# Experts fed with their own tokens in tiles of 32 slots, weights staged by GpSimd, key rows zeroed in pieces, one block's query rows loaded behind all key rows

## Chip, core and metric

One Trainium2 chip, one NeuronCore of it. The metric is the device time of one execution in microseconds (us). TensorE (PE) runs at one of two clock levels, 1.2 and 2.4 GHz; the profile gives the granted clock as a share of the higher one.

## What is computed

A transformer layer on x of 2048 tokens x 128, float32: causal attention with 16 heads of 8 (rotary), residual, layer norm; then non-causal attention and a top-1 mixture of 8 experts, with residuals and a last layer norm.

```python
# attention 1 (causal), over S = 2048 tokens, H = 16 heads, D_K = 8
Q, K, V = x@Wq.T, x@Wk.T, x@Wv.T;  Q, K = rope(Q), rope(K)
x = layernorm(x + softmax(mask(Q K^T / sqrt(8))) V @ Wo.T)
# "ffn" block: attention 2 (not causal) and the experts, D = 128, HID = 512, E = 8
t = x + msa(layernorm(x)*ln1_w + ln1_b)
xf = layernorm(t)*ln2_w + ln2_b
e = argmax(xf @ gate_w + gate_b)              # one expert for each token
y = gelu(xf @ w1[e]) @ w2[e]                  # 128 -> 512 -> 128
x = layernorm(x + t + y)
```

## The kernel before

**Stages.** The 2048 tokens are four blocks of 512 (`NB = 4`, `BLK = 512`; a block is `TB = 4` tiles of 128). The head of the program projects Q, K and V of all blocks. Q and K are split into two parts, written to DRAM (`q_scratch`, `k_scratch`), and read back several times as the rows of `query_rows` (`QA`, two blocks at a time) and `key_rows` (`KA`, all tokens). Then attention 1 runs over its query blocks, a short passage prepares attention 2, attention 2 runs over its four query blocks, and a tail does what is left of the last block.

**A step of attention.** A query block has four groups of four heads; a group has one step for each 128 keys (16 steps in attention 2, so 64 steps a block). In a step PE computes two score products (L381, `ps<-query_rows,key_rows`), ScalarE turns them into exponentials (`exps`, L782, two instructions of 128x1024), and PE multiplies the exponentials of the step before with the values (`ps<-probs,values`). The values products have 9 output columns each and are put at four column offsets of the array (0, 32, 64, 96). Three pairs of PSUM banks hold scores, so ScalarE can be fed about one step ahead. At a group's end VectorE copies the sum (`evac`), PE turns it in step 3 of the next group (`turn`), and VectorE normalises (`norm`).

**Work in the shade of attention 2.** While PE runs attention 2 of block qb, it also does the experts of block qb-1 (`side2`, a table from step to work, one PSUM bank, number 7). Steps 5 and 7: output projection; 10: turn of the normalised rows; 11: gate; 13: turn of the one-hot rows; 14 to 17: eight masks, one for each expert (`m_masks`, evacuated by `masks` on VectorE, L1220); from step 20 on (`UNIT_AT`) eight units of eight expert products each, spread over five steps a unit (`m_products`). Every expert is applied to all 512 tokens: VectorE and GpSimd multiply the token columns by the expert's mask in turn (`products`, L1231 and L896), and PE accumulates the eight masked products. So a block takes 64 products of 128x512 in float32, each with a 128x128 weight tile, which SP brings in eight loads of 512 KB through a ring (`expert_weights`, L350). A float32 product shows as two records in the profile. Four ScalarE tanh of 128x512 a block make the gelu. Block 3's experts run alone in the tail (`at_once`).

**The head.** GpSimd first zeroes the unused rows of `key_rows` in two memsets of 32x16384 (L900), then fills `values` with ones, then runs `split_k` for each block; ScalarE's first work waits for GpSimd's first sum. SP's queue waits for the two memsets (`rows_clear`), then puts ones in one row of `key_rows` (`ld_pad`), loads small weights and x, and then for each block b: stores its q and k parts, waits until they have landed, loads that block's key rows (four DMAs of 256 KB), and for b < 2 its query rows (eight DMAs of 128 KB). PE starts attention 1 when the key rows of block 0, the query rows of block 0, `ld_pad` and the shift row (`c_row`, issued by ScalarE) are there. ScalarE's work for block 3 waits for the stores of block 1.

## Time and profile before

| | us |
|---|---|
| median of 3 runs (lowest, highest) | 1318.41 (1308.98, 1332.99) |
| the profiled execution | 1305.86 |
| its span, first to last instruction | 1304.0 |

| engine | busy us | share of the span |
|---|---|---|
| PE matmul | 1097.7 | 84% |
| ScalarE | 775.0 | 59% |
| VectorE | 437.5 | 34% |
| GpSimd | 244.8 | 19% |

The busy share is a mean over stages with different limits, and a matmul's end is modelled, so it says which engine is full only together with the waits of a stage. The granted clock was 0.907 over the span. The rows below have start and duration in us; `[0.34 <-X]` behind a row is idle time before it and what ended it.

### The profile page before, as it was taken

The numbers are of one execution on the slowest core, as the hardware profiler recorded it, in microseconds if no ns is written. First come the engines' busy times: TensorE is split into PE (matmuls) and PEld (weight loads), VectorE is DVE, ScalarE is ACT, GpSimd is POOL, SyncE is SP. The second block draws the span as 40 slices with busy tenths as digits, with TensorE's granted clock in tenths as the row PEclk, the third lists the DMA queues.
The fourth block names the chain that finished last, engine by engine and source line by source line (L and its number), as shares of the span: only waits on it lengthen the run. The fifth ranks groups of instructions, "written<-read, shape, count | busy, mean of one in ns | idle before, by whom it ended". The sixth has DMA issues, their size and how long they took to land.

```text
span 1304.0 us, 22822 instructions
## 1 busy us (share of the span) xinstructions
PE 1097.7 (84%) x9300; PEld 444.8 (34%) x9300; DVE 437.5 (34%) x1074; ACT 775.0 (59%) x874; POOL 244.8 (19%) x274
## 2 busy tenths in 40 slices
PE   3408879899889639999999999899999899996667
PEld 1204334334334213333333333333333333333223
DVE  3541251510520360000434221444321534323765
ACT  0206658779779409999756567766567766562000
POOL 9203111110100000000022221022220022220334
PEclk8758798989999758999889899999999899998789
DMA  4766202000061151001001012001100001110010
GB/s 111 147 107 118 35 33 35 34 2 3 27 87 27 25 98 50 1 2 24 12 17 33 17 33 57 11 25 34 33 26 26 1 25 33 33 33 17 24 49 24
DMA packets 52922, 49.88 MB, mean 38 GB/s; under 512 B 3536, under 2 KB 39248, under 8 KB 52816
## 3 DMA queue, kind: packets, MB, share of 16 engines
q1 hardware_dynamic: 52752, 48.33, 17.9%
q8 instruction: 75, 1.23, 0.4%
q14 instruction: 31, 0.25, 0.1%
q10 hardware_dynamic: 64, 0.07, 0.0%
HBM read 38.56 MB, written 9.44 MB: 37 GB/s over the span
## 4 chain that ended last, share of the span: by engine, by line
PE 74%; DVE 13%; DMA 4%; issue 3%; POOL 2%; ACT 2%; SPq 2%; DVEq 0%; ACTq 0%; POOLq 0%
PE ps L381 71%; PE ps L386 3%; POOL key_rows L900 2%; DMA k_scratch<-parts 2%; ACT probs L782 2%; DMA query_rows<-neg_shift_final 2%; DVE early_late L1220 1%; DVE row_low L1191 1%; DVE early_late L1231 1%; DVE squares_blockdiag L1252 1%; DVE early_late L1260 1%; DVE ln_stats L961 1%; DVE ln_newton L956 0%; DVE ln_newton L954 0%; DVE squares_blockdiag L1253 0%
## 5 line engine op out<-in xcount | busy, mean ns | idle before, releaser
L782 ACT ACTIVATE probs<-ps 128x1024 f32<-128x1024 f32 (+3 forms) x832 | 751.7, 1003 | 327.0 <-PE ps L381 324.9
L381 PE MATMUL ps<-probs,values 128*9 128x256 f32 (+1 forms) x6528 | 443.8, 386 | 7.2 <-DVE q_rotated L1108 7.0
L381 PE MATMUL ps<-query_rows,key_rows 33*128 33x512 f32 (+3 forms) x1664 | 328.6, 462 | 39.4 <-DMA query_rows<-neg_shift_final 30.2
L381 PE MATMUL ps<-early_late,parts 128*128 128x512 f32 x512 | 261.8, 636 | 29.6 <-DVE early_late L1231 28.0
L381 PEld LDWEIGHTS ps<-query_rows,key_rows 33*128 33x128 f32 x1664 | 139.4, 192 | 261.1 <-issue 137.4
L381 PEld LDWEIGHTS ps<-probs,values 128*9 128x9 f32 x6528 | 145.6, 91 | 233.7 <-issue 136.3
L896 POOL TENSOR_TENSOR early_late<-h_cols,early_late 128x512 f32<-128x512 f32 x64 | 74.9, 1173 | 499.9 <-DVE early_late L1220 330.5
L381 PEld LDWEIGHTS ps<-early_late,parts 128*128 128x128 f32 x512 | 90.0, 196 | 154.3 <-issue 143.0
L875 POOL TENSOR_SCALAR_AFFINE_SELECT probs<-probs 128x256 f32<-128x256 f32 x128 | 52.2, 409 | 309.3 <-ACT probs L782 306.9
L896 POOL TENSOR_TENSOR early_late<-early_late 128x512 f32<-128x512 f32 x64 | 74.6, 1166 | 176.6 <-PE ps L381 176.1
L1108 DVE COPY q_rotated<-ps 128x512 f32<-128x512 f32 x32 | 22.1, 691 | 234.3 <-PE ps L381 234.1
L1231 DVE TENSOR_TENSOR early_late<-early_late 128x512 f32<-128x512 f32 x64 | 48.2, 763 | 111.3 <-PE ps L381 111.2
L1231 DVE TENSOR_TENSOR early_late<-h_cols,early_late 128x512 f32<-128x512 f32 x64 | 46.8, 744 | 96.1 <-PE ps L381 95.9
L796 ACT ACTIVATE squares_blockdiag<-squares_blockdiag 128x512 f32<-128x512 f32 x16 | 10.1, 631 | 73.7 <-DVE squares_blockdiag L1254 73.7
L1115 DVE RECIPROCAL recip<-ps 128x16 f32<-128x16 f32 x32 | 8.2, 258 | 92.7 <-PE ps L386 92.6
L1220 DVE CAST early_late<-ps 128x512 bf16<-128x512 f32 x32 | 22.1, 692 | 25.3 <-PE ps L381 25.1
L1191 DVE TENSOR_REDUCE row_low<-ps 128x8 f32<-128x512 f32 x32 | 22.1, 692 | 22.0 <-PE ps L381 21.8
L381 PE MATMUL ps<-early_late,w_attn 128*128 128x512 f32 x32 | 19.1, 753 | 10.1 <-DMA early_late<-in_sin 6.5
L900 POOL MEMSET key_rows<- 32x16384 f32 x2 | 27.5, 13744 | 0.3 <-POOLq L1404 0.3
L381 PE MATMUL ps<-row_bound,parts 8*128 8x512 bf16 x32 | 15.4, 489 | 11.8 <-DVE early_late L1220 10.4
L381 PE MATMUL ps<-squares_blockdiag,blk 128*16 128x512 bf16 x8 | 3.7, 461 | 23.3 <-ACT squares_blockdiag L815 23.3
L381 PE MATMUL ps<-squares_blockdiag 128*128 128x512 bf16 x32 | 13.0, 421 | 11.6 <-DVE row_low L1191 11.0
(137 smaller groups left out, 464.9 us busy)
## 6 DMA issues: line engine op xcount, KB each, us to landing
parts<-in_w SPq DMA_DIRECT2D x32, 512.0 KB, 3.8
query_rows<-q_scratch SPq DMA_DIRECT2D x64, 128.0 KB
key_rows<-k_scratch SPq DMA_DIRECT2D x20, 256.0 KB, 7.3
q_scratch<-parts SPq DMA_DIRECT2D x8, 512.0 KB, 5.8
k_scratch<-parts SPq DMA_DIRECT2D x8, 512.0 KB, 5.7
key_rows<-k_scratch SPq DMA_DIRECT2D x16, 192.0 KB, 7.0
early_late<-in_xT SPq DMA_DIRECT2D x4, 256.0 KB, 5.2
early_late<-in_cos SPq DMA_DIRECT2D x4, 256.0 KB, 5.4
```

The costliest lines, as they stand in the source:

```text
L381: return nc.tensor.matmul(out, l, r, start=start, stop=stop, skip_group_check=True)
L386: last = nc.tensor.transpose(out[0:m, i * P:(i + 1) * P], rows(i), ident[:, :])
L782: nc.scalar.activation(Pr[:, i % 2, 2 * p:2 * p + 2, lo:BLK], score_banks(t, p)[:, :, lo:BLK], ACT.Exp, scale=SCALE).then_inc(s["exp"], 1)
L875: nc.gpsimd.affine_select(out=at, in_=at, compare_op=ALU.is_ge, fill=0.0, base=0, pattern=[[0, 2], [1, P]], channel_multiplier=-1).then_in ...
L896: nc.gpsimd.tensor_tensor(prod[:, n % PSLOTS, :], hT[:, :] if c < TB else hid[:, c - TB, :], ms[:, e, :], ALU.mult).then_inc(m_pp, 1)
L900: link(nc.gpsimd.memset(KA[at:at + ROWS, :].bitcast(F32), 0.0))
L961: ins = nc.vector.bn_stats(st[:, i, :], src[:, i, :])
L1108: copy(accs[:, :], sums).then_inc(s["evac"], 1)
L1191: mark(nc.vector.tensor_reduce(low[:, t, hs], low_bank(b, i, c).rearrange("p (h t) -> p h t", t=NSUB), AX.X, ALU.max), low_taken, 2 * t + ...
L1220: mark(copy(ms[:, e, :], mask_bank(b, e)), m_ms, b * E + e + 1)
L1231: tt(prod[:, n % PSLOTS, :], hT[:, :] if u < TB else hid[:, u - TB, :], ms[:, e, :], ALU.mult).then_inc(m_pd, 1)
L1252: link(tt(t, x, x, ALU.mult))
```

## The change

**Experts.** Tokens are sorted by expert into 768 slots (`SORTED`), in `NT = 24` tiles of `TS = 32` slots, each tile with one expert. On PE `m_ranks` (step 13) replaces the turn of the one-hot rows; VectorE works out each token's slot (`dest`) and each tile's expert (`owner`). GpSimd sends the 512 rows to DRAM in four indirect DMAs (`rows_sent`), SP loads the 768 sorted rows (`sorted_rows`), and PE turns them (steps 24 and 25). Then six rounds of four tiles: `up` (four products with 32 stationary columns, 512 moving), `turn` (four transposes), `down` (16 products with 32 stationary columns, 128 moving), at steps `UP_AT`, +5 and +7. The four tiles of a round stand at column offsets 0, 32, 64, 96. The weights of all experts lie in SBUF (W1 in `parts`, W2 in `early_late`, loaded once by SP, 4 MB); for every round GpSimd reads four tile owners into registers and copies four tiles of w1 and four of w2 to `expert_stage` (in the tail ScalarE copies w1). At the block's end GpSimd stores the results and fetches 512 rows back by four indirect DMAs; VectorE adds them in the next block (`add_experts(qb - 2)`, ahead of `route`). Masks, masked products, and the weight ring are gone.

**Head.** The two memsets are cut into four pieces each of 32x4096; GpSimd does a pair of pieces ahead of each `split_k`. SP's ones in `key_rows` and the query rows of block 1 move behind the key rows of all blocks; three stores of zeros to `z_sorted` are added.

```diff
-UNIT_AT = (20, 25, 30, 36, 41, 46, 52, 57)
-TANH_AT = {28: 0, 33: 1, 38: 2, 44: 3}
+UP_AT = (26, 32, 38, 44, 50, 56)
+SORTED_AT = (24, 25)
+TANH_AT = {at + 2: r for r, at in enumerate(UP_AT)}
+IN_SHADE = side_order(UP_AT, 5, 7)
+AT_END = side_order(tuple(30 + 6 * r for r in range(ROUNDS)), 8, 13)
 # SP
-            sp.wait_ge(rows_clear, 1)
-            for at in (ROWS, HALF + ROWS):
-                sp.dma_start(kaf[at:at + 1, :, :]..., onesf...).then_inc(ld_pad, 16)
                 key_rows(1, slice(0, PAIRS), b * BLK, (b + 1) * BLK, A[1]["k_rows"][b % 2])
-                if b < 2:
+                if b == 0:
                     query_rows(1, b)
+            query_rows(1, 1)
+            sp.wait_ge(rows_clear, 1)
+            for at in (ROWS, HALF + ROWS):
+                sp.dma_start(kaf[at:at + 1, :, :]..., onesf...).then_inc(ld_pad, 16)
+            def sorted_rows(b):
+                sp.wait_ge(m_sent, 16 * TB * (b + 1))
+                sp.dma_start(zsl, z_sorted.rearrange("(r p) d -> p r d", p=P)).then_inc(m_sorted, 16)
 # PE
+            def m_up(b, k, r):
+                pe.wait_ge(m_w1, 4 * (b * ROUNDS + r + 1))
+                side_free(b, k, 2)
+                for g in range(4):
+                    last = mm(ps[g * TS:(g + 1) * TS, side_bank(b, k), :], slots(4 * r + g), w1s[g])
+            def m_down(b, k, r):
+                pe.wait_ge(m_w2, 4 * (b * ROUNDS + r + 1))
+                for c in range(TB):
+                    for g in range(4):
+                        last = mm(ps[g * TS:(g + 1) * TS, side_bank(b, k), 0:D], hTs2[...],
+                                  w2s[g][:, c * P:(c + 1) * P], c == 0, c == TB - 1)
 # GpSimd
+            def rows_sent(b):
+                pool.wait_ge(m_dest, b + 1)
+                for i in range(TB):
+                    nc.gpsimd.indirect_dma_start(out=z_sorted, ..., in_=zb[:, i, :], ...).then_inc(m_sent, 16)
+            def rows_back(b):
+                for r in range(ROUNDS):
+                    mine = [pool.value_load(owner[0:1, t:t + 1], ...) for t in range(4 * r, 4 * r + 4)]
+                    if b < NB - 1:
+                        if r:
+                            pool.wait_ge(m_side, ... ("up", r - 1))
+                        for g, e in enumerate(mine):
+                            nc.gpsimd.tensor_copy(w1s[g], W1[:, bass.ds(e * HID, HID)]).then_inc(m_w1, 1)
+                    if r:
+                        pool.wait_ge(m_side, ... ("down", r - 1))
+                    for g, e in enumerate(mine):
+                        nc.gpsimd.tensor_copy(w2s[g], W2[:, bass.ds(e * HID, HID)]).then_inc(m_w2, 1)
+                ... two stores to y_sorted, wait m_stored, four indirect DMAs back to zb
 # VectorE
+            def experts(b, order, due):
+                ... "up": copy(xg[r % 2], side), gelu_arg(b, r) (2 ops)
+                ... "turn": gelu(b, r) (1 op), copy(hTs2[:, :], side)
+                ... "down": ts(yS[:, r, :], side[:, 0:D], 0.5, None, ALU.mult)
```

SP's queue in the head, before, from block 1's stores on: its key rows, its query rows, and then block 2's stores.

```order
L271 DMA q_scratch<-parts 128x2x512 [waits a1_q_split]
L271 DMA k_scratch<-parts 128x2x512 [waits a1_k_split]
L280 DMA key_rows<-k_scratch 16x8x512 [waits a1_parts_out1]
L280 DMA key_rows<-k_scratch 16x8x512 x3
L288 DMA query_rows<-q_scratch 8x8x512 x8
L271 DMA q_scratch<-parts 128x2x512 [waits a1_q_split]
L271 DMA k_scratch<-parts 128x2x512 [waits a1_k_split]
```

And the end of the same part now, block 3 and what follows it:

```order
L305 DMA q_scratch<-parts 128x2x512 [waits a1_q_split]
L305 DMA k_scratch<-parts 128x2x512 [waits a1_k_split]
L314 DMA key_rows<-k_scratch 16x8x512 [waits a1_k_rows1,a1_parts_out1]
L314 DMA key_rows<-k_scratch 16x8x512 x3
L322 DMA query_rows<-q_scratch 8x8x512 x8
L355 DMA key_rows<-ones_f 1x128x128 [waits rows_clear]
```

The query rows of block 1 moved behind the key rows of block 3, and the ones (`ld_pad`) behind them.

PE in attention 2 beside block 0's experts, before: one step of scores and values, and two masked products behind it.

```order
L381 MATMUL ps<-query_rows,key_rows 128x512 [waits a2_exp]
L381 MATMUL ps<-query_rows,key_rows 128x512
L381 MATMUL ps<-query_rows,key_rows 128x512 [waits a2_exp]
L381 MATMUL ps<-query_rows,key_rows 128x512
L381 MATMUL ps<-probs,values 9x256 [waits a2_exp]
L381 MATMUL ps<-probs,values 9x256 x3
L381 MATMUL ps<-probs,values 9x256 [waits a2_exp]
L381 MATMUL ps<-probs,values 9x256 x3
L381 MATMUL ps<-early_late,parts 128x512 [waits m_prod_dve]
L381 MATMUL ps<-early_late,parts 128x512 [waits m_prod_pool]
```

The same place now, `up` of one round and the start of `down` of the round before one step later (a round's other steps hold only attention):

```order
L422 MATMUL ps<-expert_stage,h_cols 32x512 [waits m_side_taken,a2_norm,m_w1_staged]
L422 MATMUL ps<-expert_stage,h_cols 32x512 x3
L422 MATMUL ps<-query_rows,key_rows 128x512 [waits a2_exp]
L422 MATMUL ps<-query_rows,key_rows 128x512
L422 MATMUL ps<-query_rows,key_rows 128x512 [waits a2_exp]
L422 MATMUL ps<-query_rows,key_rows 128x512
L422 MATMUL ps<-probs,values 9x256 [waits a2_exp]
L422 MATMUL ps<-probs,values 9x256 x3
L422 MATMUL ps<-expert_stage,k_work 32x128 [waits m_side_taken,a2_norm,m_w2_staged]
L422 MATMUL ps<-expert_stage,k_work 32x128 x2
```

In place of one or two wide products behind nearly every step stand groups of narrow ones behind three steps in six, and they wait for GpSimd's copies. GpSimd's queue there, before and now (first round of block 0):

```order
L922 COPY values<-early_late 128x256x8 [waits a2_v_taken]
L896 TENSOR_TENSOR early_late<-h_cols,early_late 128x512 [waits m_mask,v_moved]
L896 TENSOR_TENSOR early_late<-h_cols,early_late 128x512
L896 TENSOR_TENSOR early_late<-h_cols,early_late 128x512 [waits m_mm] x14
L896 TENSOR_TENSOR early_late<-early_late 128x512 [waits m_hid,m_mm] x16
```

```order
L1001 COPY values<-early_late 128x256x8 [waits a2_v_taken]
L944 DMA z_sorted<-z_rows,row_shift 768x128 [waits z_clear,m_dest,v_moved]
L944 DMA z_sorted<-z_rows,row_shift 768x128 x3
L954 TENSOR_LOAD row_shift [waits ld_m,m_owner]
L954 ISA x2
L954 TENSOR_LOAD row_shift
L954 ISA x2
```

Four register loads, four copies of w1 and four of w2 a round took the place of the masked multiplications.

## Rows read from the trace of the kernel before

**Rows 1.** The page, part 4: chain that ended last, its largest lines.

```profile
PE 74%; DVE 13%; DMA 4%; issue 3%; POOL 2%; ACT 2%; SPq 2%; DVEq 0%; ACTq 0%; POOLq 0%
```

**Rows 2.** Windows: us, busy PE, PEld, DVE, ACT, POOL (count), clock, DMA share, GB/s.

```profile
490.37:611.76 121.39, 119.94 (x1300) 47.59 (x1300) 6.52 (x17) 118.79 (x131) 0.00 (x0) 0.97 0.06 15
611.76:803.00 191.24, 183.00 (x1422) 68.36 (x1420) 60.56 (x128) 121.78 (x129) 37.10 (x32) 0.94 0.11 26
...
1185.30:1304.00 118.70, 76.72 (x216) 32.88 (x215) 75.18 (x165) 4.50 (x7) 38.23 (x32) 0.84 0.10 29
```

**Rows 3.** Timeline, steps of attention 2 block 0, without experts.

```profile
509.38 0.73 PE L381 MATMUL ps<-query_rows,key_rows 33*128 33x512 f32 x4
...
510.04 1.05 PE L381 MATMUL ps<-probs,values 128*9 128x256 f32 x16
...
511.02 0.73 PE L381 MATMUL ps<-query_rows,key_rows 33*128 33x512 f32 x4
```

**Rows 4.** Timeline, one step of block 1 with two expert products.

```profile
674.23 0.73 PE L381 MATMUL ps<-query_rows,key_rows 33*128 33x512 f32 x4
...
675.87 1.98 PE L381 MATMUL ps<-early_late,parts 128*128 128x512 f32 x4
...
677.79 0.73 PE L381 MATMUL ps<-query_rows,key_rows 33*128 33x512 f32 x4
```

**Rows 5.** Timeline, block 1: a turn at step 3, and the first mask, end of step 14.

```profile
616.77 0.66 PE L386 MATMUL ps<-ident,q_rotated 128*128 128x128 f32 x4
...
640.00 0.38 PE L381 MATMUL ps<-row_bound,parts 8*128 8x512 bf16 x1
```

**Rows 6.** Groups of instructions by form: busy us, mean ns | idle before.

```profile
L896 POOL TENSOR_TENSOR early_late<-h_cols,early_late 128x512 f32<-128x512 f32 x64 | 74.9, 1173 | 499.9 <-DVE early_late L1220 330.5 <-PE ps L381 169.4
L900 POOL MEMSET key_rows<- 32x16384 f32 x2 | 27.5, 13744 | 0.3 <-POOLq L1404 0.3
L796 ACT ACTIVATE squares_blockdiag<-squares_blockdiag 128x512 f32<-128x512 f32 x16 | 10.1, 631 | 73.7 <-DVE squares_blockdiag L1254 73.7
L922 POOL COPY values<-early_late 128x2048 f32<-128x2048 f32 x1 | 1.9, 1893 | 0.0
```

**Rows 7.** Chain of waits near 87 us: a register load on VectorE's queue; the shift row.

```profile
86.88 0.56 DVEq L1071
87.47 0.20 DVEq L1071
...
89.71 10.64 DMA query_rows<-neg_shift_final
```

**Rows 8.** Timeline of SP's queue in the head: issue times.

```profile
39.88 0.47 SPq L271 DMA_DIRECT2D k_scratch<-parts  x1
45.89 2.60 SPq L280 DMA_DIRECT2D key_rows<-k_scratch  x4
...
74.98 2.51 SPq L280 DMA_DIRECT2D key_rows<-k_scratch  x4
...
103.96 2.51 SPq L280 DMA_DIRECT2D key_rows<-k_scratch  x4
...
117.40 2.48 SPq L280 DMA_DIRECT2D key_rows<-k_scratch  x4
```

**Rows 9.** Windows at the end of the head's transfers (columns as in rows 2).

```profile
117.40:127.00 9.60, 8.99 (x106) 4.48 (x107) 2.73 (x7) 7.72 (x12) 4.61 (x12) 1.00 0.89 110
127.00:134.00 7.00, 2.57 (x40) 1.30 (x32) 1.03 (x4) 1.85 (x4) 1.89 (x5) 0.84 0.03 6
```

**Rows 10.** Timeline of the head: a small VectorE cast while GpSimd zeroes.

```profile
0.80 27.55 POOL L900 MEMSET key_rows<- 32x16384 f32 x2 [0.29 <-POOLq L1404]
...
6.73 7.85 DVE L1346 CAST blk<-blk_f 128x16 bf16<-128x16 f32 x1 [4.75 <-DMA ident<-in_ident]
```

**Rows 11.** Timeline of the tail: the one-hot's turn, the last store.

```profile
1204.98 1.01 PE L386 MATMUL ps<-ident,onehot 128*8 128x128 f32 x4 [2.31 <-DVE onehot L1212]
...
1301.27 0.38 SPq L354 DMA_DIRECT2D out<-x_rows  x1
```

More of the change, by code:

```diff
@@ L638, in group @@
+            side_op = dict(sorted=m_sorted_turn, up=m_up, turn=m_hid_turn, down=m_down)
             def group(a, qb, g, side, after, before):
@@ L706, in after2 @@
                 b = qb - 1
-                first = {0: (m_xadd, b)} if b else {}
-                return {**first, 1: (m_ms, (b + 1) * E), 2: (m_ev, b * 2 * TB + 3), 3: (m_ev, b * 2 * TB + 6)}
+                first = {0: (m_taken, b * OPS)} if b else {}
+                late = {g: (m_taken, b * OPS + sum(at < g * (S // P) + TURN_STEP for at, _, _ in IN_SHADE)) for g in (2, 3)}
+                return {**first, 1: (m_dest, b + 1), **late}
             def side0(a):
@@ L1263, in experts @@
[L1263 to L1275 removed]
+                link(ins)
@@ new lines, in route @@
+                if b == 0:
+                    dve.wait_ge(ld_k, 16)
+                    link(nc.vector.memset(cum[:, 0, :], 0.0))
+                for i in range(TB):
+                    ins = tt(cum[:, i + 1, :], cum[:, i, :], oh[:, i, :], ALU.add)
+                    if i < TB - 1:
+                        link(ins)
+                ins.then_inc(m_oh, 1)
+                dve.wait_ge(m_rank, b + 1)
+                count = ps[:, 7, TB * E:(TB + 1) * E]
+                marks = wide[:, 0:E * BLK // TS].rearrange("p (e k) -> p e k", e=E)
@@ new lines, in experts @@
+            def experts(b, order, due):
+                for k, (at, name, r) in enumerate(order):
+                    if name == "turn":
+                        due(at - 1)
+                        gelu(b, r)
+                    due(at)
+                    n = b * OPS + k + 1
+                    dve.wait_ge(m_side, n)
+                    side = ps[:, side_bank(b, k), :]
+                    if name == "sorted":
+                        c = sorted_cols(r)
+                        mark(ts(c, side[:, 0:c.shape[1]], ln[:, 2:3], ln[:, 3:4], ALU.mult, ALU.add), m_taken, n)
+                    elif name == "up":
+                        mark(copy(xg[r % 2], side), m_taken, n)
+                        gelu_arg(b, r)
+                    elif name == "turn":
+                        mark(copy(hTs2[:, :], side), m_taken, n)
+                    else:
+                        mark(ts(yS[:, r, :], side[:, 0:D], 0.5, None, ALU.mult), m_taken, n)
@@ L1359, in _ @@
             b = NB - 1
+            add_experts(b - 1)
             route(b)
-            masks(b, 0, E)
             finish(b - 1)
-            experts(b, at_once)
+            experts(b, AT_END, at_once)
             add_experts(b)
```

333 lines of the change are left out of this document (170 added, 163 removed).

## Prediction

> **What bounds the kernel now.** I read the page's chain first, then the windows by stage, then the timeline inside a stage. PE holds 74% of the chain [rows 1], so the question is what PE waits for in each stage. Block 0 of attention 2 has no experts beside it: 121.4 us for 64 steps, with ScalarE busy for 118.8 [rows 2]. There ScalarE sets the pace, 118.8 / 64 = 1.86 us a step, while PE alone needs 511.02 - 509.38 = 1.64 us a step [rows 3]. Block 1, with block 0's experts beside it, takes 191.2 us at 121.8 us of ScalarE work and 183.0 of PE [rows 2]: there PE is the bound. A step with two expert products lasts 677.79 - 674.23 = 3.56 us [rows 4], that is 1.64 + 1.92. Blocks 2 and 3 look the same (I count three such blocks at 191.2). The tail of 118.7 us is one block's experts alone. The head, up to the first step of attention 1, is DMA time: the issues of the key rows are 29.1, 29.0 and 13.4 us apart [rows 8], each waiting for stores that stand behind the transfers before.
>
> **The three shaded blocks.** I build the new length of a block from its steps.
>
> Steps 0 to 13 change little. Before they ran from 611.76 [rows 2] to the first mask at 640.00 [rows 5], 28.2 us. `add_experts` puts one VectorE operation of about 0.7 us ahead of `route`, on which PE's turn at step 10 waits, and four small additions (about 0.2 us each) stand ahead of `m_ranks`: 29.7 us.
>
> Steps 14 to 23 held eight masks and the first products; they now hold nothing but the sorting on other engines. Pace of ScalarE: 10 x 1.86 = 18.6 us.
>
> Steps 24 to 63 hold six rounds of six steps. A round adds up, turn and down to PE. Turn: four transposes, 0.6 us [rows 5]. Up: four float32 products of 512 columns, eight records. Two such products (four records) take 1.92 us one behind the other [rows 4], so eight records would be 3.8 us. But the values products, which stand at four column offsets as these do, put 16 records of 256 columns into 0.98 us (510.04 to 511.02 [rows 3]), where serial they would need 16 x 0.24 = 3.8: nearly four at a time. So up is 0.95 us. Down is 16 products of 128 columns in 32 records: overlapped 1.0, serial 32 x 0.12 = 3.8; each needs its own small weight load, so I take 1.6. A round adds 3.15 us.
> The Trainium skill (TensorEngine Tiling (Array Packing), Tiling Modes and Performance Considerations) says that four 128x32 tiles run in parallel, with some 60 cycles of overhead for each product. By it up would be 0.95 as well and down nearer 1.6 than 1.0.
> If PE could always run ahead, a round would be 6 x 1.64 + 3.15 = 13.0 us. With scores only one step ahead I count the three loaded steps at PE's pace (4.9 + 3.15) and the three free ones at ScalarE's (5.6), 13.6 us. Six rounds are 81.6 us; the four steps left over, two turns of sorted rows and the group turns are 8.3, and waits for `evac` behind the gelu operations at steps 33 to 34 about 1.
> Sum: 29.7 + 18.6 + 81.6 + 8.3 + 1 = 139.2 us. Three blocks save 3 x (191.2 - 139.2) = **156 us**. Bounds: 131 (down at 1.0, full run-ahead, no evac wait) and 164 (up and down serial) a block.
>
> This is only so if nobody is late. Two chains have to fit.
> (1) Sorting. The slots are known some 3 us behind step 13. Then come four indirect DMAs from GpSimd, their landing, SP's load of 384 KB, and PE's turn at step 24, ten steps or 19 us later. No row has an indirect DMA. Lower bound: an SP issue, 0.6 us each, 2.5 us for four [rows 8]. Upper bound: 3 us each. I take 1.2: 3 + 4.8 + 2 + 3.5 = 13 us, hidden. At 3 us each it is 20.5 and PE stands 1 to 2 us.
> (2) Staging. GpSimd's copy of 2048 columns took 1.89 us [rows 6], so 512 take about 0.55. A register load on VectorE's queue cost 0.56 + 0.20 = 0.8 us [rows 7]. A round is 4 x 0.8 + 8 x 0.55 = 7.6 us against a window of five steps, about 11 us (down of one round to up of the next but one). Hidden. At 1.17 us a copy, the price of a GpSimd multiplication [rows 6], it is 12.6 and PE would stand about 1.7 us a round.
> ScalarE gets two more tanh a block, 1.3 us at 0.63 [rows 6], hidden while PE bounds. SP has fewer loads; its wait for the sent rows holds up only `rows_out` and the next shift row, due a block later.
>
> **The tail.** The one-hot rows are ready at 1204.98 [rows 11]. Now: add_experts 0.7, counts 0.8, ranks 1.0 (four transposes cost 1.01 there [rows 11]), slots 2.0, four sends 4.8 and landing 2.0, load 3.2, turn and evacuation 2.0: first up at 1221.5. Before, the first product stood at about the same place. Then rounds: w1 has one buffer, so ScalarE starts four register loads and four copies when the last up is done; I take 4 x 1.2 + 1.0 for up = 5.9 us. Last up 1222.5 + 5 x 5.9 = 1252; gelu, turn, down 7.5; store 3.3; fetch 6.8; add 0.7; layer norm 5.1; last store's issue at 1275.5, against 1301.27 before [rows 11]. With the round still open I put **24.5 us** saved; bounds 10 (3 us a DMA, 8 us a round) and 35.
>
> **The head.** GpSimd no longer holds up the start. The two memsets took 27.5 us [rows 6]; with a quarter of them ahead (6.9 us), block 0's stores can be issued when VectorE and ScalarE are through, near 20.5 instead of 39.9 [rows 8]. Later blocks need their split 29 us apart, and 6.9 + 4 us of GpSimd fit. But the transfers remain. Block 0's stores to its key rows 6.0 us; key rows, query rows and stores 29.1; without query rows 13.4; so query rows alone are 15.7, and the last key rows 9.6, when the DMA share falls from 0.89 to 0.03 [rows 8, 9]. Now in a row: 6 + 29.1 + 13.4 + 13.4 + 9.6 + 15.7 = 87.2, and `ld_pad` stands behind all of it, some 3 us. PE waits for `ld_pad` before its first product, so attention 1 starts at 20.5 + 90 = 111 instead of 100.4 (where the shift row landed, 89.71 + 10.64 [rows 7]). Before, block 1's query rows and the keys of blocks 2 and 3 still moved while PE worked. I put **+10.5 us**; bounds -8 (ring rates a fifth better) and +15.
> The Trainium skill (SBUF — State Buffer, "The 'DVE blocks DMA' trap") says that GpSimd and VectorE lock a shared port out for whole instructions. The trace agrees: a cast of 16 columns took 7.85 us and ended with the first memset [rows 10].
>
> **Sum.** 1304.0 - 156 - 24.5 + 10.5 = 1134; 1.9 us lie outside the span: 1136 for an execution like the profiled one (1305.86). The median of the runs shown is 1.0% above that one; I go half of it up and predict **1141 us**.
>
> **Rivals.**
> (A) Staging is late, 15%. Copies at 1.17 us make PE wait 1.7 us in each of 18 rounds (31 us) and sends of 3 us add 5 in the blocks and 9 in the tail. 1141 + 45 = 1186. For it: GpSimd's multiplications run at 1.17 and VectorE gets in its way. Against: a plain copy ran at half of that.
> The Trainium skill (SBUF — State Buffer, the same section) says that DMAs issued from GpSimd starve while VectorE holds that port; no row here has such a DMA, and by it time would move to this rival.
> (B) The narrow products don't overlap: up and down at 3.8 each, 25 us a block and some in the tail, 1141 + 80 = 1221; 5%. Against it: [rows 3].
> (C) The head gains: with the transfers at better rates, or attention 1 quicker since nothing moves beside it, it starts at 92, 19 us below my sum, and the tail is at its best: 1112; 17%.
> (D) Slower than before: GpSimd becomes the bound. To pass 1318 x 1.02 the 24 rounds would have to take 8.5 us more each than in my sum, 13.6 + 8.5 = 22 us for a round of twelve GpSimd operations, 1.85 us each. The dearest row is 1.17, so 3%; then some 1350.
> (E) The experts' saving is eaten elsewhere, within 2%: sorting so late (over 60 us a block) that PE stands. Chain (1) would have to be four times my sum; 2%.
> My forecast has 58%.
>
> **Range.** The forecast's own: blocks 3 x 5, tail 10, head 8, run to run 8; about 1115 to 1170. To hold 8 in 10 it reaches to (C) and towards (A): 1108 to 1178. A difference under 2% can't be told from none in this kernel. Faster 0.95, same 0.02, slower 0.03.
>
> **What would show it.** Three stretches of attention 2 with experts at 136 to 143 us, PE busy over 90% of each at a clock of at least 0.95; steps 14 to 23 at 1.86 us. No PE idle before the sorted turn at step 24 or before up (else A). Up about 1 us for eight records, down 1.6 (else B). GpSimd's copy 0.55. First product of attention 1 near 111, released by the ones of `key_rows`, with SP's first store near 20 (else C). Last up to last store about 23 us. Wrong would be: PE idle behind GpSimd's copies, a clock that falls in the shade, or a block over 165.

## The result, and the profile after

The changed kernel took 1136.11 us in the median of 4 runs (1127.68 to 1151.96), beside 1314.34 us for the kernel before on the same chip: a ratio of 0.863, with a 95% interval of 0.857 to 0.869. Some executions of a kernel are slow ones, over 1.5% above its fastest: the ratios leave them out, and the profiled executions of `spread` (1131.41 us) and `tail_order` (1140.23) are such. The execution profiled has a span of 1125.9 us; the one before had 1304.0. The chain of work that ended last, by engine:

```profile
PE 66%; DVE 11%; DMA 9%; ACT 5%; issue 4%; SPq 2%; POOL 1%; another core or an unknown queue 1%; POOLq 0%; ACTq 0%; DVEq 0%
```

PE has fallen from 74% of the chain [rows 1] to 66% and VectorE from 13% to 11%; the DMAs have risen from 4% to 9%. The windows of the kernel after, by stage (columns as in [rows 2]): the head, attention 1, the passage, attention 2's blocks 0 to 3, the tail.

```profile
0.00:107.60 107.60, 30.03 (x110) 14.96 (x110) 37.27 (x88) 11.96 (x21) 40.47 (x22) 0.67 0.74 149
107.60:452.00 344.40, 308.68 (x3255) 135.42 (x3261) 91.10 (x265) 263.83 (x320) 51.90 (x127) 0.92 0.15 27
452.00:501.60 49.60, 15.94 (x70) 8.60 (x67) 31.34 (x106) 3.49 (x7) 3.51 (x4) 0.65 0.45 81
501.60:623.00 121.40, 119.91 (x1304) 47.74 (x1308) 6.50 (x17) 118.98 (x131) 0.00 (x0) 0.97 0.13 39
623.00:757.20 134.20, 130.40 (x1594) 57.70 (x1586) 43.15 (x117) 122.57 (x135) 35.21 (x54) 1.00 0.08 17
757.20:892.70 135.50, 130.65 (x1596) 57.91 (x1594) 51.03 (x141) 122.62 (x135) 38.95 (x58) 1.00 0.10 20
892.70:1027.70 135.00, 129.84 (x1596) 57.54 (x1594) 51.56 (x141) 121.08 (x133) 38.95 (x58) 1.00 0.04 13
1027.70:1125.90 98.20, 34.91 (x302) 20.56 (x302) 50.07 (x152) 18.34 (x30) 30.93 (x38) 0.56 0.08 23
```

Against [rows 2]: block 0 is the same. The three shaded blocks run from 623.0 to 1027.7, 404.7 us, where they ran from 611.76 to 1185.3, 573.5: **168.8 us saved**. The tail went from 118.7 to 98.2: **20.5 saved**. Attention 1 starts at 107.6 instead of 100.4: **7.2 lost**. Between there and the start of attention 2's block 0 another **4.0** were lost. In all -168.8 - 20.5 + 7.2 + 4.0 = -178.1, the difference of the spans. PE is busy for 96 to 97% of a shaded block, at full clock; in the tail for 36%, at 0.56.

### The profile page after: what moved, and what is told of

It is laid out like the page before. It is cut to its first block, busy times and chain, and to the rows that moved or that the text cites. A ratio compares the mean times of both kernels' runs of the same rounds, so it can differ in the third digit from the quotient of the medians.

```text
span 1125.9 us, 24400 instructions
## 1 busy us (share of the span) xinstructions
PE 900.4 (80%) x9813; PEld 400.4 (36%) x9820; DVE 362.0 (32%) x1027; ACT 782.9 (70%) x906; POOL 239.9 (21%) x360
## 4 chain that ended last, share of the span: by engine, by line
PE 66%; DVE 11%; DMA 9%; ACT 5%; issue 4%; SPq 2%; POOL 1%; another core or an unknown queue 1%; POOLq 0%; ACTq 0%; DVEq 0%
PE ps L422 61%; DMA k_scratch<-parts 4%; ACT probs L829 4%; PE ps L427 3%; DMA key_rows<-ones_f 2%; DVE row_low L1273 1%; PE ps L675 1%; DMA y_sorted<-early_late 1%; DMA query_rows<-neg_shift_final 1%; SPq L322 1%; ACT squares_blockdiag L843 1%; DMA z_rows<-y_sorted,row_shift 1%; POOL z_rows L970 1%; SPq L314 1%
## 5 line engine op out<-in xcount | busy, mean ns | idle before, releaser
L422 PE MATMUL ps<-query_rows,key_rows 33*128 33x512 f32 (+3 forms) x1664 | 337.0, 465 | 73.1 <-DMA key_rows<-ones_f 42.6
L963 POOL COPY expert_stage<-early_late 128x512 f32 x72 | 45.4, 668 | 162.1 <-PE ps L422 162.1
L944 POOL DMA_INDIRECT z_sorted<-z_rows,row_shift x16 | 15.8, 990 | 237.3 <-issue 177.0
L959 POOL COPY expert_stage<-parts 128x512 f32 x72 | 47.9, 707 | 44.6 <-PE ps L422 39.1
L900 ACT ACTIVATE expert_stage<-parts 128x512 f32 x24 | 15.1, 630 | 48.7 <-DVE row_shift L1322 27.6
L1354 DVE COPY k_work<-ps 128x512 f32<-128x512 f32 x24 | 16.6, 690 | 62.9 <-PE ps L675 62.9
L422 PE MATMUL ps<-expert_stage,k_work 128*32 128x128 f32 x576 | 29.3, 301 | 4.1 <-issue 2.4
L422 PEld LDWEIGHTS ps<-expert_stage,k_work 128*32 128x32 f32 x576 | 24.2, 122 | 13.6 <-issue 6.2
L422 PE MATMUL ps<-early_late,w_attn 128*128 128x512 f32 x32 | 19.9, 780 | 11.4 <-DMA early_late<-in_sin 7.3
L422 PE MATMUL ps<-early_late,k_work 128*32 128x128 f32 x192 | 29.0, 301 | 0.0
L984 POOL MEMSET key_rows<- 32x4096 f32 x8 | 28.0, 3504 | 0.9 <-POOL row_ok L974 0.5
L422 PE MATMUL ps<-expert_stage,h_cols 128*32 128x512 f32 x128 | 20.2, 709 | 4.4 <-ACT expert_stage L900 3.3
## 6 DMA issues: line engine op xcount, KB each, us to landing
query_rows<-q_scratch SPq DMA_DIRECT2D x64, 128.0 KB
```

What stands on the lines that cost most here:

```text
L422: return nc.tensor.matmul(out, l, r, start=start, stop=stop, skip_group_check=True)
L900: nc.scalar.activation(w1s[g], W1[:, bass.ds(e * HID, HID)], ACT.Copy).then_inc(m_w1, 1)
L944: nc.gpsimd.indirect_dma_start(out=z_sorted, out_offset=bass.IndirectOffsetOnAxis(ap=dest[:, i:i + 1], axis=0), in_=zb[:, i, :], in_offset ...
L959: nc.gpsimd.tensor_copy(w1s[g], W1[:, bass.ds(e * HID, HID)]).then_inc(m_w1, 1)
L963: nc.gpsimd.tensor_copy(w2s[g], W2[:, bass.ds(e * HID, HID)]).then_inc(m_w2, 1)
L984: link(nc.gpsimd.memset(KA[at:at + ROWS, part].bitcast(F32), 0.0))
```

## Experiments

Ratios are to the kernel before, run beside each, with their 95% interval in brackets; the changed kernel's is 0.863. "Block" is the time from one gate product to the next in the trace: the two shaded stretches are 195.8 and 191.0 us in the kernel before, 135.6 and 135.0 in the changed one, and the stretch from the last shaded one into the tail is 180.4 and 128.0.

### What the blocks' 169 us were: columns on TensorE

`narrow_products`, on the kernel before:

```diff
+                    wide = BLK if e == 0 else P
-                    mm(unit_bank(b, u), wring[:, (n // E) % WSLOTS, e, :], prod[:, n % PSLOTS, :], ...
+                    mm(unit_bank(b, u)[:, 0:wide], wring[:, (n // E) % WSLOTS, e, :], prod[:, n % PSLOTS, 0:wide], ...
```

> The kernel before with seven of every eight expert products on 128 columns instead of 512 (the output leaves out those experts for three quarters of the tokens); masks, masked copies, loads and waits are all there. Theory 1 (the product's columns on TensorE priced the shaded block, 0.86 us each): 56 x 0.64 = 36 us less in each of three blocks and 0 to 25 in the tail, 1312 - 108 - 12 = about 1190 us (1180 to 1215). Theory 2 (the masked copies on VectorE and GpSimd, 1.9 us for two, or the waits for masks carried the block): under 15 us a block, over 1265 us.

It took 1202.96 us, ratio 0.915 (0.909 to 0.921). The gate's products in its timeline:

```profile
801.41 1.06 PE L381 MATMUL ps<-gate_w,h_cols 128*128 128x8 f32 x8
...
962.17 1.06 PE L381 MATMUL ps<-gate_w,h_cols 128*128 128x8 f32 x8
```

They are 160.8 us apart, against 191.0: 30.3 less there and 35.4 in the block ahead, with every masked copy, mask, load and wait in place. So the columns priced the block, at 30 to 35 of the 36 us worked out.

`full_width`, on the changed kernel:

```diff
-                    last = mm(ps[g * TS:(g + 1) * TS, side_bank(b, k), :], slots(4 * r + g), w1s[g])
+                    last = mm(ps[:, side_bank(b, k), :], sorted_cols(r // 4)[:, r % 4 * P:(r % 4 + 1) * P], w1s[g], g == 0, g == 3)
...
-                        last = mm(ps[g * TS:(g + 1) * TS, side_bank(b, k), 0:D], hTs2[:, c * P + g * TS:c * P + (g + 1) * TS],
-                                  w2s[g][:, c * P:(c + 1) * P], c == 0, c == TB - 1)
+                        last = mm(ps[:, side_bank(b, k), 0:D], hTs2[:, c * P:(c + 1) * P],
+                                  w2s[g][:, c * P:(c + 1) * P], c == 0 and g == 0, c == TB - 1 and g == 3)
```

> The changed kernel with each expert product on all 128 columns of its round instead of on its tile's 32: the four products of a step are added up in one bank, so the output is no longer the reference's from there on (each slot gets the sum over its round's four tiles' experts). Same number of products, same columns streamed, but no two of them beside each other. Theory 1 (narrow tiles overlap four times, and TensorE's time carries the block): up goes from 0.97 to 3.4 us, down from about 0.95 to 3.4, so 4.5 to 5 us more in each of 18 shaded rounds and 5 to 9 in the tail's 6 at half clock: 1136 + 85 + 40 = about 1260 us (1230 to 1290), a shaded round 17.5 us instead of 12.9. Theory 2 (ScalarE's pace carries the block, TensorE has room): under 30 us more.

It took 1258.54 us, ratio 0.963 (0.955 to 0.970). Its timeline, two ups of one block:

```profile
703.71 3.70 PE L422 MATMUL ps<-expert_stage,h_cols 128*128 128x512 f32 x8
...
722.25 3.70 PE L422 MATMUL ps<-expert_stage,h_cols 128*128 128x512 f32 x8
```

A round is 18.5 us here. In the changed kernel the same eight records take 1.04 us, and down's 32 take 0.99, from their first at 701.79 to the score product behind them at 702.78:

```profile
699.28 1.04 PE L422 MATMUL ps<-expert_stage,h_cols 128*32 128x512 f32 x8
...
701.79 0.29 PE L422 MATMUL ps<-expert_stage,k_work 128*32 128x128 f32 x3
...
702.57 0.27 PE L422 MATMUL ps<-early_late,k_work 128*32 128x128 f32 x1
702.78 0.73 PE L422 MATMUL ps<-query_rows,key_rows 33*128 33x512 f32 x4
```

The same number of products over the same moving columns, with four beside each other or with none, differs by 122 us. The weights of `full_width` are wider too (128 stationary columns instead of 32), but a record costs 3.70 / 8 = 0.46 us there, no more than one of the old products with the same weights (1.98 / 4 = 0.50 [rows 4]), so it is the overlap that is gone. Without the overlap the change would still have been faster than before, but by 4%.

### What the head's 7 us were: the place of the ones

`before_head` is the kernel before with only the head of the change: the value memset first, the key rows zeroed in pairs of pieces, block 1's query rows and the ones behind all key rows.

> The kernel before with only the head of the change: the values' ones first, key rows zeroed in four pairs of pieces between the key splits, the ones and block 1's query rows behind all key rows. Theory 1 (the prediction's head term): slower by 7 to 11 us, attention 1 starts at 108 to 111 instead of 100.4. Theory 2 (the head term is right but only beside the sorting's other changes, or it is a gain): no change or faster by 5 us and more.

1324.93 us, ratio 1.010 (1.003 to 1.017): a small loss, 12 us by the medians. Attention 1 starts at 110.18, released by the ones. By itself this part of the change costs time.

`query_back`, the changed kernel with block 1's query rows loaded where they were before:

```diff
-                if b == 0:
+                if b < 2:
                     query_rows(1, b)
-            query_rows(1, 1)
             sp.wait_ge(rows_clear, 1)
```

> The changed kernel with block 1's query rows loaded behind block 1's key rows again, as before, the ones still last. Theory 1 (what is behind the ones matters, not the order ahead of them): the sum of transfers ahead of the ones is the same, so within 3 us of the changed kernel, 1133 to 1139 us. Theory 2 (the order of the query rows is what the head's loss or gain comes from): 5 to 10 us more or less.

1132.48 us, ratio 0.864 (0.859 to 0.869): no difference. Attention 1 starts at 104.2, still on the ones. The order ahead of them hardly matters. What they stand behind does:

`pads_early`:

```diff
+                if b == 1:
+                    sp.wait_ge(rows_clear, 1)
+                    for at in (ROWS, HALF + ROWS):
+                        sp.dma_start(... the ones ...).then_inc(ld_pad, 16)
             query_rows(1, 1)
-            sp.wait_ge(rows_clear, 1)
-            for at in (ROWS, HALF + ROWS):
-                sp.dma_start(... the ones ...).then_inc(ld_pad, 16)
```

> The changed kernel, with the wait for the zeroed key rows and the two transfers of ones moved from behind all key rows to right behind block 1's key rows (query rows of block 1 stay behind all key rows). Theory 1, the place of the ones behind everything sets the start of attention 1: in the changed kernel it starts at 107.6 us, the ones issued at 88.5. Issued at about 56 and landing within 3 to 19 us they let it start at 70 to 76, block 0 of attention 1 (24 us) is over at about 97, and block 1 waits for its query rows until about 105 instead of starting at 132: 25 to 32 us less in all, 1104 to 1111 us. Theory 2, the volume of the head's transfers sets it (87 us of them one behind another): attention 1 starts early, but its first blocks wait for rows and less than 10 us are gained, 1126 to 1136 us.

1105.28 us, ratio 0.842 (0.836 to 0.848), **31 us less than the changed kernel** by the medians, 28 by the ratios. First the changed kernel's SP queue and first product of attention 1, then those of `pads_early`:

```profile
53.40 2.50 SPq L314 DMA_DIRECT2D key_rows<-k_scratch  x4
...
87.88 1.26 SPq L355 DMA_DIRECT2D key_rows<-ones_f  x2
```

```profile
107.59 1.54 PE L422 MATMUL ps<-query_rows,key_rows 33*128 33x512 f32 x6 [42.60 <-DMA key_rows<-ones_f]
```

```profile
54.50 2.72 SPq L355 DMA_DIRECT2D key_rows<-ones_f  x2
```

```profile
69.02 1.54 PE L423 MATMUL ps<-query_rows,key_rows 33*128 33x512 f32 x6 [5.47 <-DMA query_rows<-neg_shift_final]
...
108.51 1.22 PE L423 MATMUL ps<-query_rows,key_rows 33*128 33x512 f32 x4 [10.65 <-DMA query_rows<-neg_shift_final]
```

PE stood 42.6 us for two rows of ones whose operands were ready at about 50 (the last memset ends at 49.5); 38.6 of them were the ones' alone, since the shift row lets PE start at 69.0. It is the place that makes them late: behind the eight loads of query rows the second landed 19.0 us after its issue in the changed kernel (88.5 to 107.5), and 9.6 in `pads_early`. Issued early, they let block 0 of attention 1 run beside the other blocks' transfers, and block 1 waits 10.65 us for its shift row, where it waited 4.86 in the changed kernel.

### Staging: hidden, but with little to spare

`stage_twice`:

```diff
+                            link(nc.gpsimd.tensor_copy(w1s[g], W1[:, bass.ds(e * HID, HID)]))
                             nc.gpsimd.tensor_copy(w1s[g], W1[:, bass.ds(e * HID, HID)]).then_inc(m_w1, 1)
...
+                        link(nc.gpsimd.tensor_copy(w2s[g], W2[:, bass.ds(e * HID, HID)]))
                         nc.gpsimd.tensor_copy(w2s[g], W2[:, bass.ds(e * HID, HID)]).then_inc(m_w2, 1)
```

> The changed kernel with every expert weight copy on GpSimd done twice, one behind the other (5.3 us of copies a round become 10.7 to 11, in the three shaded blocks; in the tail only the second weights). Theory 1 (staging is hidden in a round of 12.9 us, and neither its end nor the port it shares with VectorE is on the path): shaded blocks within 2 us of 135 each, the tail 0 to 10 us longer, 1136 to 1146 us. Theory 2 (staging or the shared port is nearly the bound, the prediction's rival A): up or down wait for staged weights, 3 us and more a round, over 1165 us.

1197.92 us, ratio 0.914 (0.909 to 0.919). My theory 1 was wrong here: it is 62 us more. Its timeline, and its windows (columns as in [rows 2]) without a wait and from one up to the next:

```profile
701.76 1.07 PE L422 MATMUL ps<-expert_stage,h_cols 128*32 128x512 f32 x8 [1.36 <-POOL expert_stage L960]
...
717.62 1.94 PE L422 MATMUL ps<-expert_stage,h_cols 128*32 128x512 f32 x8 [2.79 <-POOL expert_stage L960]
...
736.51 1.06 PE L422 MATMUL ps<-expert_stage,early_late 128*32 128x512 f32 x8 [2.73 <-POOL expert_stage L960]
```

```profile
682.00:696.00 14.00, 13.72 (x184) 6.29 (x176) 4.78 (x10) 12.20 (x15) 4.98 (x9) 1.00 0.00 1
...
701.76:717.62 15.86, 12.84 (x165) 5.47 (x165) 3.79 (x6) 11.73 (x13) 9.82 (x16) 0.99 0.01 2
717.62:736.51 18.89, 15.92 (x165) 6.52 (x165) 4.37 (x7) 11.93 (x13) 9.81 (x16) 0.82 0.00 1
736.51:755.43 18.92, 15.13 (x168) 6.21 (x168) 4.80 (x10) 11.84 (x13) 9.81 (x16) 0.90 0.01 3
```

GpSimd copies a round's second weights when the down of the round before is done, and behind them the next round's first weights. So its window is the stretch from that down to the next up. In the changed kernel this is 9.3 us (702.84 to 712.15), or 10.4 where a group turn stands in it, and not the 11 of the prediction; the eight copies take 5.4 of it (703.04 to 708.47). Doubled they took 12.0 us (705.54 to 717.56), and PE waited 1.4 to 3.1 us before up, 12 times in the three shaded blocks (and up to 3.1 us before down five times in the tail).

The wait is only about half of the price. Between the ups of rounds 2 and 3 the clock stayed at 0.99 and the time rose from 12.87 to 15.86 us, the 3 us of the wait. Between those of rounds 3 and 4 it rose from 12.90 to 18.89, at a clock of 0.82: up, 1.04 us before, takes 1.94 in the row at 717.62, and the down that GpSimd waits for comes later too (its copies start 6.8 us behind up instead of 3.8). A block, from gate to gate, went from 135.6 to 153.5 us: 17.9 more, of which the waits before up are 9.7. Rival A was real. By these rows its threshold lies near 4 us more of copies a round (an estimate, 9.3 - 5.4).

### The tail: a right round for a wrong reason

`tail_sets` gives the tail four sets of first weights:

```diff
+        w1t = [V[:, 0:4 * HID].rearrange("p (g n) -> p g n", g=4), Pr[:, 0], Pr[:, 1]]
...
-                    if r:
-                        act.wait_ge(m_side, ... .index(("up", r - 1)))
+                    if r >= 4:
+                        act.wait_ge(m_side, ... .index(("up", r - 4)))
```

> The changed kernel with four sets of staged first weights in the tail (values and exponentials are free there), so that ScalarE's copies don't wait for the up products of the round before. Theory 1 (the copies carry the tail's round, as the prediction had it): the rounds fall from 5.9 us to the 4.4 to 4.9 of VectorE's and TensorE's own work, 5 to 9 us less, 1127 to 1131 us. Theory 2 (the chain up, VectorE, tanh, turn, down carries the round at half clock): under 3 us.

1134.73 us, ratio 0.861 (0.855 to 0.867): no difference that can be told from none. From the sorted rows' turn to the last turn the trace shows 40.6 us against 42.5, and the turns still come every 6.3 us. Its PE and VectorE in one round:

```profile
1087.30 1.11 PE L681 MATMUL ps<-ident,q_work 128*128 128x128 f32 x4 [1.64 <-DVE q_work L1341]
1088.35 1.94 PE L428 MATMUL ps<-probs,h_cols 128*32 128x512 f32 x8
```

```profile
1090.42 0.69 DVE L1357 COPY q_work<-ps 128x512 f32<-128x512 f32 x1 [1.27 <-PE ps L428]
1091.14 0.69 DVE L1333 TENSOR_TENSOR squares_blockdiag<-q_work 128x512 f32<-128x512 f32 x1
1091.87 0.69 DVE L1334 SCALAR_TENSOR_TENSOR squares_blockdiag<-squares_blockdiag,q_work 128x512 f32<-128x512 f32 x1
1092.48 0.28 DVE L1362 TENSOR_SCALAR early_late<-ps 128x128 f32<-128x128 f32 x1
1092.80 0.78 DVE L1341 SCALAR_TENSOR_TENSOR early_late<-squares_blockdiag,early_late 128x512 f32<-128x512 f32 x1
```

```profile
1093.63 1.12 PE L681 MATMUL ps<-ident,early_late 128*128 128x128 f32 x4 [1.64 <-DVE early_late L1341]
```

This is the chain: turn, the up of the round after next, then VectorE takes that up, squares it, multiplies, takes down, and only then (L1341) finishes the gelu that the next turn waits for, though its tanh was long there. `tail_order` moves it:

```diff
-                    if name == "turn":
+                    if name == "turn" and (b < NB - 1 or r == ROUNDS - 1):
                         due(at - 1)
                         gelu(b, r)
+                    if name == "up" and b == NB - 1 and r:
+                        gelu(b, r - 1)
```

> tail_sets with one more edit: in the tail VectorE finishes a round's gelu ahead of the next round's up, instead of behind that up's three operations and the down of the round before. In tail_sets the turns still came every 6.3 us at half clock, though ScalarE's staging no longer waited. Theory 1 (the in-order chain turn 1.1, up 1.94, then VectorE's copy, two products, down's copy and gelu 3.7, carries the tail's round): a round falls to TensorE's 4.6 to 5.0 us at half clock, 6 to 9 us less than tail_sets, 1125 to 1129 us. Theory 2 (TensorE's half clock and staging by GpSimd carry it): within 3 us of tail_sets, turns still 6 us and more apart.

1122.88 us, ratio 0.854 (0.850 to 0.858), 12 less than `tail_sets` by the medians, 9 by the ratios, with intervals that just overlap. Its turns:

```profile
1097.92 0.82 PE L681 MATMUL ps<-ident,q_work 128*128 128x128 f32 x4
...
1102.14 0.66 PE L681 MATMUL ps<-ident,early_late 128*128 128x128 f32 x4
1102.73 1.06 PE L428 MATMUL ps<-expert_stage,early_late 128*32 128x512 f32 x8
```

They are 4.2 us apart, and PE doesn't wait before them. From the sorted rows' turn to the last turn it is 31.3 us, and 32.4 and 31.6 in `best` and `final` below, which have the same tail. The tail got more than I expected, since PE, now with fewer gaps, is granted its full clock for some rounds (turn 0.66 us instead of 1.12, up 1.06 instead of 1.94). The order and the clock can be told apart: `all_three` below has the tail of `tail_sets`, and took 36.7 us for the stretch at a clock of 0.73, where `best` took 32.4 at 0.71. So some 4 of the 9 us are the order of work at a like clock, and the rest comes with the clock. VectorE is now the full engine, busy for 13.4 of the 14.1 us from 1097.92 to 1112. How much of the gain is there without the further weight sets of `tail_sets` was not tried.

### The round's clump, and all together

`spread`:

```diff
-UP_AT = (26, 32, 38, 44, 50, 56)
-SORTED_AT = (24, 25)
+UP_AT = (25, 31, 37, 43, 49, 55)
+SORTED_AT = (23, 24)
...
-IN_SHADE = side_order(UP_AT, 5, 7)
+IN_SHADE = side_order(UP_AT, 4, 8)
```

> The changed kernel with the expert work of a shaded round in steps 0, 2 and 4 of its six instead of in three neighbouring ones (up one step earlier, turn 4 and down 8 steps behind it). Theory 1 (the clump: three steps in a row in which TensorE has 2.2 to 2.6 us of work against ScalarE's 1.86 empty the score banks, and ScalarE waits 0.56 us twice a round): a round falls from 12.87 us toward ScalarE's 11.8, TensorE's sum being 12.35; 0.5 to 0.9 us in each of 18 rounds, so 8 to 16 us less, 1120 to 1128. Theory 2 (TensorE's sum carries the round wherever its parts stand): within 4 us of the changed kernel.

1126.55 us, ratio 0.854 (0.848 to 0.860): some 10 us less by the medians, with intervals that overlap. The stretch from the last shaded block into the tail fell from 128.0 to 125.4, and `final` below has blocks of 132.4 and 132.3 us instead of 135.6 and 135.0. So the clump cost some 2.6 us a block, about 8 in all: the low end of theory 1. The spread kernel's second shaded stretch shows something else. It is 142.5 us long, 10 more than in `final`; its turn at step 10, and the windows around it (columns as in [rows 2]):

```profile
774.21 0.66 PE L427 MATMUL ps<-ident,z_rows 128*128 128x128 f32 x4 [2.41 <-DVE z_rows L1051]
```

```profile
768.00:776.00 8.00, 5.59 (x64) 2.21 (x58) 6.12 (x27) 5.61 (x7) 0.00 (x0) 0.95 0.00 1
776.00:784.00 8.00, 8.00 (x56) 3.82 (x52) 3.00 (x23) 4.36 (x5) 0.00 (x0) 0.50 0.01 2
784.00:792.00 8.00, 8.00 (x56) 2.97 (x48) 2.78 (x11) 4.82 (x6) 2.37 (x3) 0.50 0.04 15
792.00:800.00 8.00, 8.00 (x56) 2.66 (x56) 2.38 (x13) 5.04 (x6) 6.05 (x10) 0.50 0.22 67
```

PE waits at step 10 for rows that VectorE norms behind `add_experts`, and right behind it the clock is 0.50 for 27 us. The same wait stands in the ten traces of sorting kernels with narrow products. In block 1, which has no `add_experts`, it is 0.70 us, ten times, and the clock never fell there. In blocks 2 and 3 it is 1.42 to 2.41 us, twenty times, and seven times the clock fell to half at its end, for 3 to 27 us (once each in `spread`, `best`, `all_three`, `tail_sets` and `pads_early`, twice in `tail_order`). A fall of 20 us and more cost some 9 to 12 us, by the three stretches from gate to gate against those of a trace with the same block and no fall. So the addition seems to cost 0.7 us and more of waiting and, in some executions, some 10 us of clock; no run took the addition away to show it.

`all_three` (spread, the four sets, the ones behind block 1's key and query rows):

> The changed kernel with spread, tail_sets and the head of pads_early, block 1's query rows moved back behind block 1's key rows. Theory 1 (the three bounds lie in different stages and their gains add up; block 1 of attention 1 no longer waits 10.7 us for a shift row queued behind its query rows, 5 us more than pads_early): 1136 - 31 - 12 - 7 - 5 = about 1081 us (1074 to 1092). Theory 2 (the later stages take part of it back): 1095 to 1105 us.

1094.94 us, ratio 0.832 (0.827 to 0.836), at the low end of theory 2's range, but for another reason: attention 1 started at 80.3, not at 69. The ones stood behind block 1's query rows and landed 18.8 us after their issue. `best` puts them ahead of these query rows and adds `tail_order`'s edit:

> all_three with tail_order's edit and with the ones ahead of block 1's query rows again (in all_three they stood behind them, landed 18.8 us after their issue, and attention 1 began at 80.3 instead of 69.0). Theory 1: attention 1 begins at 69 to 70, block 1 follows at 94 to 104; 6 to 10 us from the head and 5 to 8 from the tail: 1079 to 1084 us. Theory 2 (the head's volume gives the earlier start back in block 1's waits): 1086 to 1091 us.

1088.32 us, ratio 0.827 (0.825 to 0.830). This is in theory 2's range. Attention 1 started at 78.7, now waiting for block 0's shift row: issued at 68.3, it landed 10.3 us later, beside the query rows. Last, `final` is `best` with block 1's query rows behind all key rows:

> best with the head of pads_early as it stood: block 1's query rows behind all key rows. Theory 1 (in best they stood between the ones and block 0's shift row, which landed late: attention 1 began at 78.7 and block 1 at 117.7, against 69.0 and 108.5 in pads_early): attention 1 begins at 69 to 70, block 1 at 108 to 109, and the 9 us are kept to the end: about 1079 us (1074 to 1084). Theory 2 (a later wait takes them back): 1085 to 1091 us, as best.

**1074.76 us, ratio 0.820 (0.816 to 0.825)**: 5% less than the changed kernel, 18% less than before. Its start of attention 1 and of its block 1:

```profile
69.45 1.54 PE L429 MATMUL ps<-query_rows,key_rows 33*128 33x512 f32 x6 [5.53 <-DMA query_rows<-neg_shift_final]
108.07 1.22 PE L429 MATMUL ps<-query_rows,key_rows 33*128 33x512 f32 x4 [8.91 <-DMA query_rows<-neg_shift_final]
```

So theory 1 holds, and the change's choice to load block 1's query rows late is right, once the ones are not behind them.

## Why the prediction was right, point by point

**The time.** Predicted 1141, measured 1136. The terms were -156, -24.5 and +10.5 against -168.8, -20.5, +7.2 and 4.0 that no term held. The mechanism of each was right in the main, but that 1141 came so near is partly luck: the blocks were 12.8 us too dear and the head 3.3, while the tail and the term that was missing make 8.0 the other way. For an execution like the profiled one the sum gave 1136, and it took 1127.68.

**Which engine bounds what.** Right: `narrow_products` and `full_width` show from both kernels that TensorE's columns carry the shaded blocks.

**The block, 139.2 forecast, 134.9 measured.** The steps up to the ranks and the sorting behind them were as drawn: the sorted rows' turn came 47.8 us into block 2 (757.2 to 804.97), 48.3 in the sum. The term that was too high is the round: 13.6 forecast, 12.87 us measured where no group turn stands in it (tanhs at 692.33, 705.20, 718.06). Of these 0.7 us, 0.6 are down: I took 1.6 between 1.0 and 3.8, and it is 0.99. The lower bound from [rows 3] was the right value. The Trainium skill (TensorEngine Tiling (Array Packing), Performance Considerations) speaks of some 60 cycles of overhead for each product, and I estimated from it that down would be nearer 1.6; the 32 records in 0.99 us show no such addition. It also says there that a product of one column takes as long as one of 60, and read so, as a floor, it doesn't lengthen products of 128 columns; with that reading the trace agrees. Six rounds 0.7 us shorter are about the 4.3 us of the block. The clump that I counted into the round was real: I had 0.6 us a round, 3.6 a block, and `spread` gave back some 2.6.

**Sorting, chain (1).** It is hidden, as said: the sorted rows' turn at step 24 (804.97) followed with no wait, 8.0 us behind the landing of the rows (796.96). An indirect DMA holds GpSimd for 0.98 us, with 0.30 between two; I took 1.2.

**Staging, chain (2).** It is hidden, as said, but both of its numbers were too high. A round's staging takes 5.4 us and not 7.6: copies take 0.61 to 0.71 us instead of 0.55, and the four register loads show as 0.4 us of idle time instead of 3.2 (as 1.7 in `stage_twice`). The groups of the changed kernel (busy us, mean ns | idle before):

```profile
L959 POOL COPY expert_stage<-parts 128x512 f32 x72 | 47.9, 707 | 44.6 <-PE ps L422 39.1 <-issue 5.5
L963 POOL COPY expert_stage<-early_late 128x512 f32 x72 | 45.4, 668 | 162.1 <-PE ps L422 162.1
```

GpSimd waits for PE, not the other way round. The window is 9.3 us and not 11. What the prediction had too low is the price behind that margin: for rival A it counted the wait alone (1.7 us a round), and in `stage_twice` waits of 9.7 us a block cost 17.9.

**The tail, 24.5 forecast, 20.5 measured.** Up to the first up the sum was exact: 36.2 us forecast from the tail's start (1221.5 - 1185.3), 1063.85 - 1027.7 = 36.15 measured. The round of 5.9 was measured as 5.8 (first to last up 28.9 us for five), but its reason failed: not ScalarE's staging with one buffer but VectorE's order of work behind up, as `tail_sets` and `tail_order` show; at half clock both chains take about 6 us. What is missing is behind the last up: I had 23.5 us from its end to the last store, and it is 28.5 (1094.71 to 1123.17), since the turn of round 4 still stands ahead of round 5's with a round between them, at half clock:

```profile
1092.77 1.94 PE L422 MATMUL ps<-expert_stage,early_late 128*32 128x512 f32 x8
...
1098.35 1.11 PE L675 MATMUL ps<-ident,early_late 128*128 128x128 f32 x4 [2.67 <-DVE early_late L1335]
...
1103.69 1.11 PE L675 MATMUL ps<-ident,q_work 128*128 128x128 f32 x4 [1.41 <-DVE q_work L1335]
```

**The head, +10.5 forecast, +7.2 measured.** The mechanism was as drawn, transfers one behind another and the ones behind all of them (`before_head` shows it by itself, +12 us by the medians). SP's first store stood at 20.9, near the 20.5, and from there to the landing of the ones it took 86.6 us instead of 90. What I did not ask is whether the ones had to stand there: 31 us lay in their place, more than the whole term.

**What no term held, 4.0 us.** In the last block of attention 1 PE stood 2.45 us with nothing in the profile to wait for, and ran at half clock behind it (the window 393 to 401 has 0.63):

```profile
395.18 1.01 PE L422 MATMUL ps<-query_rows,key_rows 33*128 33x512 f32 x3 [2.45 <-issue]
```

The same place has 2.44 us in `query_back` and 0.80 in `full_width`, which differs from the changed kernel in its expert products alone. All eleven traces of sorting kernels have this wait, 0.80 to 2.99 us, and none of the three with the old experts. In each of the eleven a packet of 16 KB on an instruction queue starts 2.9 to 3.8 us before PE goes on, while SP loads key rows. In the changed kernel the DMA view of 388 to 398 us has it (packets, MB, share); the DMA share was 1.00 and more while PE stood:

```profile
q1 hardware_dynamic: 281, 1.09, 77.8%
q8 instruction: 1, 0.02, 1.1%
```

That speaks for code that is loaded late, but the old kernels have such a packet without a wait, and no run tests it: the cause is open. Nor are the 4.0 us clear of the noise. From its first product to attention 2's, attention 1 takes 392.2 us now and 388.1 before, but 396.1 in `narrow_products`, whose code up to there is that of the kernel before.

**Rivals.** B is refuted by the 1.04 us of up; its price was too low as well, 80 us where `full_width` measured 122, since two of its shaded blocks grew by 37 and 43 us where B had 25. C, the head that gains, did not come; D and E were far off. A did not happen, but stood nearer than its price said.

## What to carry to other kernels

Ask of every load that something waits for whether it must stand where it stands in the queue: two small rows behind everything cost some 30 us, a sixth of what the whole rewrite gave. When a bound is derived from one engine's wait, look for the second chain of about the same length before removing it; here taking away the first gave nothing that could be told from noise, and the second 9 to 12 us. And a margin is not only the wait it saves: waits of 1.4 to 3 us inside an otherwise full stretch took the clock with them in `stage_twice` and cost nearly twice their length.

## What the runs showed of the hardware

- Four narrow products at four column offsets overlap almost fully even when each has only 128 columns: 32 records in 0.99 us. The same products on all columns, one behind another, take 3.70 us for up's eight records instead of 1.04.
- The store of the experts' rows that GpSimd issued at 755.79, beside SP's load of the query rows, took 8.56 us to land; in the tail, with nothing beside it, it took 2.26. `add_experts` waited 0.53 us for what followed from it. The Trainium skill (SBUF — State Buffer, "The 'DVE blocks DMA' trap") says that DMAs issued from GpSimd starve while VectorE holds the shared port. That is not what this trace shows: VectorE was busy for 1.3 of the 8.56 us, the DMA engines for 57%, and in all eleven sorting kernels the store that stands a few us behind those loads is the slow one (8.0 to 11.4 us, others up to 4.4). The 32 indirect DMAs held GpSimd for 0.95 to 1.16 us each and show no such starving either.
- TensorE's clock fell to half behind waits of 1.42 to 2.41 us in full stretches, 7 times in 20; behind waits of 0.70 us at the same place never in 10. In the shaded blocks of `stage_twice` it fell behind all eight waits of 2.7 us and more and behind none of the four of 1.4. In the tail it was at 0.56, with waits of 1.4 to 2.9 us before every turn; once `tail_order` had closed most of these, PE ran at full clock from its second turn to its fifth.
